# Attention and routing kernel on one Trainium2 core: a ring of three PSUM banks for key products and transposes, query halves beside key products, four probability buffers, value products in halves

## What is computed

```python
att = jnp.einsum('bhqd,bhkd->bhqk', q, k) / np.sqrt(HD)   # HD = 8
att = jnp.where(causal[None, None], att, -jnp.inf)
att = jax.nn.softmax(att, axis=-1)
y = jnp.einsum('bhqk,bhkd->bhqd', att, v)
y = y.transpose(0, 2, 1, 3).reshape(b, s, d)
return y @ w_out.T + b_out
...
h = _layernorm(x, axis=-1) * (1 + cb) + sb                # then the experts' logits, choice and slots
```

## Time and profile before

| | |
|---|---|
| median of 3 runs | 956.09 us (951.81 to 960.04) |
| the profiled execution | 952.5 us |
| its span, first to last instruction | 950.5 us |
| PE busy | 728.3 us (77%) |
| DVE busy | 566.9 us (60%) |
| ACT busy | 460.4 us (48%) |
| POOL busy | 394.3 us (41%) |
| mean granted TensorE clock | 0.841 of full speed |

### The profile page before, as it was taken

The page is one execution under the profiler, slowest core; times in us unless marked ns, Lnnn a source line. Parts: engine busy times, 40 slices in busy tenths (PEclk is TensorE's granted clock), DMA queues, the critical chain, the costliest instruction groups (busy, mean ns, idle before and its releaser), DMA issues.

```text
span 950.5 us, 17156 instructions
## 1 busy us (share of the span) xinstructions
PE 728.3 (77%) x5876; PEld 397.3 (42%) x5876; DVE 566.9 (60%) x1066; ACT 460.4 (48%) x903; POOL 394.3 (41%) x432
## 2 busy tenths in 40 slices
PE   4655688889979798879787979886208999999950
PEld 2332233333324223324222333222207888888850
DVE  6859588888677876777866687511603333333314
ACT  2540467777656555656554556562003444444420
POOL 5541111113152164152155153155360777777762
PEclk9975599999789977989977799765557999999985
DMA  4244723551101111101111000000023554543237
GB/s 122 76 158 158 153 66 67 97 113 36 35 2 36 35 37 47 36 2 35 35 33 49 2 2 2 2 26 21 0 62 90 89 90 90 89 87 38 26 28 182
DMA packets 68177, 55.97 MB, mean 59 GB/s; under 512 B 7040, under 2 KB 58752, under 8 KB 68096
## 3 DMA queue, kind: packets, MB, share of 16 engines
q1 hardware_dynamic: 54528, 45.40, 18.4%
q0 software_dynamic: 13568, 9.51, 7.3%
HBM read 29.19 MB, written 25.31 MB: 57 GB/s over the span
## 4 chain that ended last, share of the span: by engine, by line
PE 59%; DVE 12%; issue 8%; ACT 8%; DMA 6%; POOL 4%; SPq 2%; DVEq 0%; ACTq 0%; POOLq 0%
PE psum L858 15%; PE psum L843 13%; PE psum L1058 11%; PE psum L1082 8%; ACT prob_all L1200 7%; PE psum L818 4%; DVE mx L1392 3%; DMA k_parts<-prob_all 2%; POOL slot_rows L626 2%; PE psum L867 2%; PE psum L826 1%; DVE xn L1333 1%; DMA slot_rows<-early,idxb 1%; SPq L366 1%; PE psum L880 1%
## 5 line engine op out<-in xcount | busy, mean ns | idle before, releaser
L1200 ACT ACTIVATE prob_all<-psum 128x512 f32<-128x512 f32 x576 | 318.0, 598 | 219.2 <-PE psum L843 207.7
L1392 DVE TENSOR_REDUCE mx<-psum 128x2 f32<-128x1024 f32 (+3 forms) x384 | 347.2, 953 | 117.9 <-PE psum L818 57.5
L843 PE MATMUL psum<-stack 51*128 51x512 bf16 (+3 forms) x768 | 199.2, 365 | 64.5 <-ACT prob_all L1200 44.3
L641 POOL TENSOR_SCALAR_AFFINE_SELECT prob_all<-prob_all 128x512 f32<-128x512 f32 x128 | 79.0, 635 | 358.9 <-ACT prob_all L1200 351.8
L858 PE MATMUL psum<-prob_all,vst 128*32 128x512 f32 (+3 forms) x1536 | 181.8, 575 | 3.1 <-POOL prob_all L641 3.1
L818 PE MATMUL psum<-stack 48*128 48x512 bf16 (+3 forms) x768 | 164.9, 370 | 19.8 <-DVE mx L1392 11.7
L736 POOL DMA_INDIRECT sums<-ys,dest_of x80 | 124.6, 1558 | 81.0 <-ACT ys L1262 53.4
L843 PEld LDWEIGHTS psum<-stack 51*128 51x128 bf16 x768 | 49.4, 96 | 236.0 <-ACT prob_all L1200 165.9
L1758 DVE TENSOR_TENSOR hid<-psum,hT 128x512 f32<-128x512 f32 (+1 forms) x96 | 57.1, 602 | 94.1 <-ACT hT L1255 66.4
L626 POOL DMA_INDIRECT slot_rows<-early,idxb x64 | 62.8, 981 | 41.8 <-issue 18.4
L826 PE MATMUL psum<-mask_k,mask_q 64*128 64x64 bf16 x1024 | 75.6, 200 | 0.0
(11 more groups left out here) (178 smaller groups left out, 687.8 us busy)
## 6 DMA issues: line engine op xcount, KB each, us to landing
slot_rows<-fill SPq DMA_DIRECT2D x4, 1300.0 KB, 11.4
vals<-slot_rows SPq DMA_DIRECT2D x8, 650.0 KB
stack<-q_parts SPq DMA_DIRECT2D x32, 96.0 KB
stack<-k_parts SPq DMA_DIRECT2D x32, 96.0 KB
xs<-x SPq DMA_DIRECT2D x4, 512.0 KB, 6.4
stack<-q_parts SPq DMA_DIRECT2D x32, 64.0 KB
stack<-k_parts SPq DMA_DIRECT2D x32, 64.0 KB
early<-w1T SPq DMA_DIRECT2D x8, 256.0 KB
```

The lines of the kernel that those rows point to most:

```text
L641: ins = nc.gpsimd.affine_select(out=v, in_=v, compare_op=ALU.is_ge, fill=0.0, base=0, pattern=[[0, GH], [1, P]], channel_multiplier=-1)
L843: mm = nc.tensor.matmul(psum[:, KB[s % 2], col:col + w], kst[buf][r, hp, kb * P:kb * P + P], qst[buf][r, hp, qc * 512 + q0:qc * 512 + q0 + ...
L1200: nc.scalar.activation(probs[kind % NP][:, h, :], psum[:, KB[s % 2], :], ACT.Exp, scale=SCALE).then_inc(exped, 1)
L1392: ins = nc.vector.tensor_reduce(mx[:, part, :, hp, i], psum[:, QB[u % 2]:QB[u % 2] + 2, col:col + w], AX.X, ALU.max)
```

## The change

Five things are changed together.

1. Key units and all the transposes and small products that used bank 7 share a ring of three banks, 4, 5 and 7. A table (`ring`) lists the order of the users; each user takes the bank of the user three places before, and waits until that one has been read: by ACT's exponential for a key unit, by DVE's division (`o_norm`) for an output transpose, and so on (`take`). Slots called "none" pad the list to a multiple of three.
2. The two heads of a query unit are issued apart: head e = 1 at an even step, head e = 0 at the odd step after it, each beside the key unit that stands on the other rows. `QSTEP` becomes -12, -10, -8 and so on to 22, one unit in every two steps without a pause.
3. There are four probability buffers.
4. The value products of a kind are issued in two portions (`values_begin`, `values_end`) at the steps of `VBEGIN` and `VEND`; kind 0 stays in one piece, and kind 3 is parted at its second piece.
5. Routing work is moved by some steps, and POOL's second norm is parted: the first half at kind 2, the second at kinds 6 and 7 behind a wait on `m_step`, which DVE raises when it has split the maxima. The output is turned at steps 10 and 20 (before 9 and 22), divided at 11 and 21 (before 11 and 24), the maxima are split at step 23 (before 24).

```diff
-NP = 3
+NP = 4
...
-QSTEP = [-7 + u * 32 // NQU for u in range(NQU)]
+QSTEP = [2 * u - 12 for u in range(NQU)]
 EARLY = sum(q < 0 for q in QSTEP)
-NSTEP, MSTEP = 24, 29
+NSTEP, MSTEP = 23, 29
+COMMON = {10: ("late_out",), 20: ("early_out",), MSTEP: ("maxima",)}
+VBEGIN = [9, 11, 15, 21, 24, 28, 32, 35, None]
+VEND = [None, 13, 17, 23, 26, 30, 34, None, None]
+MIXED = [
+    {17: ("heads0",), 26: ("heads1",)},
+    {2: ("added0",), 12: ("added1",), 26: ("rows0",)},
+    {6: ("rows1",), 14: ("logits",)},
+    {7: ("prefix",)},
+]
+def ring(mix, m):
+    slots = []
+    for s in range(NKU):
+        if s == NKU - 3:
+            more = 3 + sum(len(v) for k, v in COMMON.items() if k > s)
+            slots += ["none"] * (-(len(slots) + more) % 3)
+        slots.append(s)
+        slots += (MIXED[m].get(s, ()) if mix else ()) + COMMON.get(s, ())
...
-        KB = [4, 5]
+        KB = [4, 5, 7]
...
+                    if mix and m == 1 and kind == 6:
+                        pool.wait_ge(m_step, (n + 2) * 5)
+                        second_norm(b - 1, 1)
+                    if mix and m == 1 and kind == 7:
+                        second_scale(b - 1, 1)
...
+                def take(user):
+                    i = slots.index(user)
+                    j = i - 3
+                    while j >= 0 and absent(slots[j]):
+                        j -= 3
+                    if j < 0:
+                        if not first:
+                            pe.wait_ge(exped, n * NKU + j + 1)
+                    elif isinstance(slots[j], int):
+                        pe.wait_ge(exped, n * NKU + slots[j] + 1)
+                    elif slots[j] == "late_out":
+                        pe.wait_ge(o_norm, 2 * n)
+                    elif slots[j] == "early_out":
+                        pe.wait_ge(o_norm, 2 * n + 1)
+                    elif slots[j] == "maxima":
+                        pe.wait_ge(mT_copied, n + 2)
...
                 for s in range(NKU):
-                    key_unit(n, m, s, first and s < 2)
+                    key_unit(n, m, s, take(s))
                     for u in range(NQU):
                         if QSTEP[u] == s and more > 0:
-                            query_unit(n + 1, nxt, u, False)
+                            query_half(n + 1, nxt, u, 1, False)
+                        if QSTEP[u] + 1 == s and more > 0:
+                            query_half(n + 1, nxt, u, 0, True).then_inc(q_scores, 1)
...
-                    if s % 4 == 3 and s >= 7:
-                        kind = s // 4 - 1
-                        if kind == 0:
-                            after(pe, o_copied, 2 * n)
-                        if kind == 3:
-                            pe.wait_ge(o_copied, 2 * n + 1)
-                        values(n, m % 2, kind)
+                    for kind in range(NK):
+                        if VBEGIN[kind] == s:
+                            values_begin(n, m, kind)
+                        if VEND[kind] == s:
+                            values_end(m, kind)
```

More of the change, by code:

```diff
@@ L814, in query_unit @@
                     diag = k0 + w == (i + 1) * P
[L815 to L819 removed]
+                    r = slice(64 * e, 64 * e + KR)
+                    o = psum[:, QB[u % 2] + e, col:col + w]
```

262 lines of the change are left out of this document (141 added, 121 removed).

## The result

| | before | after |
|---|---|---|
| median | 953.95 us (950.82 to 960.04) | 941.17 us (940.58 to 942.08) |
| ratio after to before | | 0.9872, 95% interval 0.9831 to 0.9912 |
| profiled execution, its span | 952.5 us, 950.5 us | 942.1 us, 940.3 us |

What follows compares the result with a forecast made beforehand. It took attention to be bound by engines holding each other up, DVE's own work the most. Terms -4.7 - 1.5 - 18.2 - 14.5 - 5.2 = -44.1 gave 908.4 us profiled, 912 us median; own range 897 to 930, wider range 883 to 945.

Steps and rivals of the forecast that it cites:

- DVE 108.7 + 4 x 3.5: Batches 1 and 2: DVE's busy time plus 3.5 us of holes a group, 122.7 us a batch before ring and clock.
- Clean groups, 27.0 us each: Groups 1 to 3, no routing: DVE 23.5 us plus 3.5 us of holes, 27.0 us against 28.57 a group.
- I take 0 for the pairing itself ... and a loss I exclude: Query heads issued beside keys on PE: worth 0, at most 3.8 us of PE a group, with no loss.
- Read-backs, 0.5 us each: Key units 13 and 23 wait for DVE's division, so DVE waits 0.5 us for scores, twice a group: 1.0 us.
- Routing's ring waits, 2 us a batch: Batches 1 and 2: ring waits for projections, logits and prefix counts, 0.5 us or less each, eight a batch, counted as 2 us.
- I keep 0.87's share, 1.3 a group: Batches 1 and 2: PE's clock stays at 0.87, costing 1.3 us a group or 5.3 us a batch.
- Rival B: Slower through PE's falling clock: a group takes 27 + 13 f us at half-speed share f; 970 us at 0.7; chance 0.07.
- POOL's 16 scatters of group m = 3 start at kind 2 as before: POOL in group m = 3: scatters start at kind 2 as before, with no gain or loss entered in the sum.
- Halves, 0.2 us a block: PE's value products: about 0.2 us change-over for each of 8 more blocks, 1.6 us more PE work a group.
- POOL's second half behind DVE's split: Routing groups: POOL's second half waits until DVE's split is done, one reason the holes around the late division go.
- (2): Check on clean groups: ACT's idle before L1200 for PE halved, in pieces under 0.6 us, none of 0.8 at each kind.
- Rival A: DVE's holes stay as wide because the ring couples key units to DVE's reading: 940 to 960 us; chance 0.12.

Runs made afterwards that it cites:

- moved wait: Changed kernel with POOL's wait for the scatters' landing moved from the end of m = 3 to m = 1 of the next batch: 932.37 us, ratio 0.9758.
- filled logits: Changed kernel, heads apart, with one idle 512-column product (zero weights) behind each of the eight logits products in m = 2: 931.94 us, ratio 0.9834.

## Why the prediction was wrong, step by step

The step that failed is the sum for the routing groups, "DVE 108.7 + 4 x 3.5", with 2 us for the ring and 5.3 us for the clock a batch, and nothing for POOL's scatters. It took DVE as the bound there with the holes of a clean group. DVE's busy time came as forecast (107.7 and 106.6 us), but it was idle 8.5, 10.5 and 9.8 us a group in the three batches, where the sum allows 5.3 in the first two. PE was busier than DVE (121 and 131 us): in group 6 33.9 us of 38.3 against 26.5, and in group 8 35.3 of 38.4 against 23.7, at clocks of 0.78 and 0.69.

- **Clean groups, 27.0 us each.** 27.17, and DVE's holes 27.16 - 23.56 = 3.6 against 3.5. Right, and largely in its parts: of the 3.5 us, 1.2 were for value blocks between the two heads of a unit, which leaves 2.3 without the pairing, and with the heads together the holes are 25.37 - 23.12 = 2.25.
- **"I take 0 for the pairing itself ... and a loss I exclude".** Of PE's work this holds; as a judgement on the part it failed. It counted PE's slots, which do stay the same, and not when a unit's second head is there. The pairing costs 1.8 us in each clean group (1.35 in DVE's holes) and 1.5 in each routing group, 2% in all (0.967 against 0.9872). The forecast's own sum had 1.2 us of it as holes, so this explains a small part of the miss; what it hid is that undoing the pairing is the better kernel. The hole where a block lies between two heads (0.2 us) was seen; that the transpose and the ring's wait lie there too was not.
- **Read-backs, 0.5 us each.** In the ring of the change key units waited 1.0 us each for the division (11.8 us, 12 times). Check (5) named the wait and its length of about 1 us; the sum had taken half of it.
- **Routing's ring waits, 2 us a batch.** From the waits of the changed kernel: 5.0 + 4.0 + 3.0 us, and 1.5 and 0.9 for the rank and the logits, 14.4 us in three batches instead of 6. The projections (L947) waited 3.9 us more for the division.
- **The clock, "I keep 0.87's share, 1.3 a group".** Over the attention the mean stayed (0.87, before 0.86), but in the 11 routing groups it fell from 0.86 to 0.84, and in m = 2 from 0.93 to 0.81. The price was too low there as well. The 12 us a unit of clock came from group 0 of before; in the m = 2 groups the runs show 16 to 25 us a unit. What sets the price stays open: PE was busy 91% of group 0 before (28.1 of 31.0 us), about as in group 8 of the changed kernel (35.3 of 38.4 us), and in group 0 of the changed kernel 0.16 of clock cost only 0.4 us. Rival B's formula (13 us for all of a group at the low level, 26 a unit) is nearest to the m = 2 groups; the forecast wrote it down and did not use it in its own sum, where a mean of 0.87 would give 3.4 us a group instead of 1.3. Rival B's limit itself rests on a slip: the 15 groups with maxima take 510.7 us (102.3 to 613.0), not 517.
- **"POOL's 16 scatters of group m = 3 start at kind 2 as before", booked at nothing.** They do start so, and their chain to the next group's masks did not get shorter (the two pairs took 155.0 us before and 153.3 after). 9 and 7 us of the miss lie in m = 3 and m = 0; moving one wait of 5.6 us returned 5.1 and 3.0 us in the two pairs.
- **Halves, 0.2 us a block.** About right. In m = 1 groups at clock 1.00 halves take 31.07 us and whole blocks 29.82 (ring, heads together), 1.25 us for 8 blocks more, 0.16 each if all of it is change-over; in clean groups halves cost nothing (27.17 against 27.33, 25.37 against 26.11). The Trainium skill, "TensorEngine Tiling (Array Packing)", Key Properties, says that changing the tiling mode drains the engine; that speaks against halves, and these m = 1 groups agree.
- **POOL's second half behind DVE's split.** Right: in group 5 of the changed kernel the operation of the earlier trace rows that had taken 1.13 us takes 0.19:

```profile
266.46 0.19 DVE L1494 SCALAR_TENSOR_TENSOR mres<-mx,mparts 128x32 f32<-128x32 f32 x1
```

The 3.83 us wait of the earlier trace rows is gone too, as check (4) said, and m = 1 groups are 2 us shorter (36.1 to 33.6 for group 5). Of the announced checks (1), (3), (4) and (5) held, and (2) did not: ACT's waits in a clean group fell only from 8.9 to 6.3 us, with pieces of up to 0.9 us. None of the three signs of being wrong appeared (clean groups that stay at 28.5 us, a clock there under 0.9, key units that wait over 2 us). Signs and checks looked mostly at the clean groups, and the miss was elsewhere.

Rival A named the ring's coupling, and its mechanism is part of what happened; rival B's price too. The result, 941 us, stands at A's near end and inside the range given (883 to 945), 29 us from the time forecast.

The 32 us by place: m = 2, 11; m = 3 and m = 0, 16; m = 1, 5. By cause they are not fully parted. In m = 2 the clock can make up 5 to 10 of the 11 us (three groups at 0.81 and 16 to 25 us a unit are 9 to 14 us, of which the forecast had 4), but in the changed kernel itself no run held the clock there. In m = 3 and m = 0 POOL's chain, the ring and the clock act together, and the runs bound the parts only one by one (moved wait 8 us, ring 10 where the wait is already moved); they are not to be added. For m = 1 ring waits and late heads are the likely cause.

## What to carry to other kernels

When two products that feed one reader are issued apart, count the time to the last of them, not the engine's slots; and a shared ring of banks makes a user wait for whoever reads the bank's last content, so a slow reader of side work holds the main chain. Here the ring paid in groups with few readers (1.4 us each) and not in those with many. A price of the clock taken from one stretch does not carry over to another: here a whole unit of it cost 12 us in group 0 before, 2.5 in group 0 after, and 16 to 25 in the m = 2 groups. Where a stretch does not shrink with the rest, look for the chain of another engine in it (here POOL's scatters and their landing) before a gain is booked.

## What the chip showed beyond that

- The clock fell behind thin products. Eight products of 8 columns in 1.95 us stood 0.7 us ahead of a fall to 1.2 GHz, and with the heads together a 512-column product behind each of them kept 2.4 GHz in groups 6, 10 and 14 of one profile, while fourteen such products ahead of and behind the stretch did not keep it with the heads apart. The Trainium skill, "TensorE: Matmul & The Clock Gate", Why this matters for your kernels, says that the clock swings with thin-M products when the loop goes to the next DMA before all K-tiles are done; these products had 8 columns and waited for no DMA, so no run here shows that case.
- The clock does not fall in the same places in every profile. Group 4 is the same in the changed kernel and in the one with filled logits, and took 29.26 us at 1.00 in one profile and 29.93 us at 0.94 in the other. The period of a single group in a single profile is therefore weak evidence, outside the clean groups at least.
- A DVE operation on 128 x 32 elements took 1.13 us beside POOL's norm and 0.19 us when POOL's second half came after it, with no change to the operation. That POOL's work beside it is the reason is read from these two times, not tested by itself.
